# First chunk of a CIN tower: rows of x by transposes on the chip instead of a trip through DRAM

## The chip, the cores and the metric

The kernel runs on one core of one Trainium2 chip. The metric is the device time of the kernel in microseconds (us). Every line number L123 is a line of the kernel before.

## The reference, cut to what matters

For each of 512 samples, 32 table rows of 32 floats are gathered by `ids`. They form x[b, h, d], with field h and embedding dimension d. Two CIN layers follow, then a small tower.

```
z   = einsum('bhd,bmd->bhmd', x, x)        # layer 0: 32 x 32 pairs of fields
x1  = relu(einsum('b(hm)d,(hm)n->bnd', z, filter_0))      # n = 128
z   = einsum('bhd,bmd->bhmd', x, x1)       # layer 1: 32 x 128 pairs
x2  = relu(einsum('b(hm)d,(hm)n->bnd', z, filter_1))
h   = concat([sum_d x1, sum_d x2, dense_ctx])             # 512 x 272
y   = relu(relu(h @ W_top1 + b_top1) @ W_top2 + b_top2) @ W_top3
```

## The kernel before, in words

**Chunks and tiles.** The work is cut into 32 chunks c. A chunk is 128 samples (block bt = c // 8) times 4 embedding dimensions, so it has 512 columns. Each chunk has four tiles q, one for each dimension, and there are 128 tiles in all.

**Layer 0 of a chunk.** The pairs of fields are rows of up to 128, and a "product" is one row of x (repeated) times another. Symmetric pairs are folded, so there are four products k = 0 to 3 of 128 rows and one small one. VectorE (DVE) multiplies (`product`, L562), ScalarE (ACT) rounds the product to fp32r (`split_high`, L453), and DVE takes the rest (`split_low`, L567). TensorE (PE) then runs three fp32r passes per product (`three_passes`, L700 to L702) into the accumulator `acc0`. The small rows take one pass (`layer0_rest`, L723). After that ACT writes `prev_hi` (L465) and DVE writes `prev_lo` (L571).

**Where the rows come from.** ACT sorts the gathered block by dimension (`sort_d`, L431), PE transposes it (`turn_x`, L709) and ACT copies it to `xt_stage` (L440). SyncE (SP) writes it to a DRAM scratch `xt` (`write_xt`, L245 and L246) and reads it back three times with repeated rows: `load_xm` (L251), `load_xb` (L256) and `load_x16` (L263). ACT copies `xm` to PSUM (`copy_xm`, L446). The queue of SP runs in program order, and loads wait until the product that read the buffer is done.

**Layer 1 of a chunk.** It consists of 8 banks for each tile. A bank is three passes of 512 columns, four fields by 128 outputs. Four or five banks of a tile go to `ya` and are scaled by ACT (`scale_bank`, L473, four ACTIVATEs for each bank) and summed by GpSimd (POOL) and an accumulating DMA (`halve`, L313, and `sum_up`, L320). The other three or four go to `yd` and are scaled and summed by DVE (`add_bank`, L614), with a lag of three tiles. So the first three tiles of chunk 0 have only ACT banks. `ya` has two buffers and `yd` has three.

**Order.** All queues are written out by hand in the order (chunk c, tile q, bank j). Layer 0 of chunk c + 1 lies between the banks of chunk c. Layer 0 of chunk 0 lies ahead of everything. POOL gathers the 32 fields of block 0, then 22 of block 1 (`EARLY_NEXT`), and the other 74 gathers lie one at a time between its sums in chunks 0 to 19. ACT sorts block 1 within chunk 5, after a wait for all its gathers. On DVE the low half of filter 1 (`w1_lo`, L551) is made ahead of layer 0 of chunk 0.

## Time and profile before

| | us |
|---|---|
| three runs | 913.08, 915.85, 915.92 (median 915.85) |
| profiled execution, its own time | 913.09 |
| its span, first to last instruction | 911.1 |
| first bank of layer 1 starts at | 80.65 |
| first `yd` bank starts at | 101.31 |

The span has three parts. In the first part x is gathered and layer 0 of chunk 0 is made, up to the first bank. The second part holds three tiles whose banks all go to ACT. In the third part both consumers work and TensorE is busy without a break until the tail.

### The profile page before, as it was taken

To read this page: it belongs to the slowest core of one execution; us is meant where nothing else is said; L and a number is where in the kernel's file an instruction comes from. 1 tells how busy PE (TensorE), PEld (TensorE's weight loads), DVE (VectorE), ACT (ScalarE), POOL (GpSimd) and SP (SyncE) were. 2 spreads that over 40 slices of the span, in tenths; PEclk is the share of its full clock that TensorE was granted. 3 is DMA by queue.
4 is the path that set the end of the run, shared out by engine and by line. 5 is a ranking of instruction groups with operands and counts; after the bars stand their busy time and mean duration, and the time that the engine had idled before them with its cause. 6 is when DMAs were issued, how large, how long until landed. Compare 5 with 4: busy or idle time off the path is not lost.

```text
span 911.1 us, 14406 instructions
## 1 busy us (share of the span) xinstructions
PE 834.5 (92%) x3580; PEld 669.8 (74%) x3580; DVE 762.5 (84%) x2394; ACT 766.9 (84%) x2577; POOL 666.2 (73%) x633
## 2 busy tenths in 40 slices
PE   0316999999999999999999999999999999999997
PEld 0113788887888888887888788887888888888773
DVE  0213699998999999998999999998999999999774
ACT  0314999999999999999999999999999999999872
POOL 6773688787879887886888888866676666676580
PEclk9998999999999999999999999999999999999999
DMA  9144766776766766768766767667676676665430
GB/s 268 19 108 129 168 149 155 163 170 166 171 150 150 164 156 155 159 145 189 164 155 143 165 144 166 157 153 169 151 168 159 153 158 154 145 155 117 79 65 0
DMA packets 57575, 133.32 MB, mean 146 GB/s; under 512 B 8770, under 2 KB 22306, under 8 KB 57395
## 3 DMA queue, kind: packets, MB, share of 16 engines
q0 software_dynamic: 22384, 68.70, 41.8%
q1 hardware_dynamic: 32178, 59.94, 20.3%
q10 hardware_dynamic: 2928, 3.76, 1.4%
q8 instruction: 28, 0.46, 0.2%
q14 instruction: 57, 0.46, 0.1%
HBM read 62.64 MB, written 5.24 MB: 75 GB/s over the span
## 4 chain that ended last, share of the span: by engine, by line
PE 84%; ACT 5%; POOL 4%; issue 3%; DVE 2%; DMA 1%; SPq 0%; DVEq 0%
PE ya L700 14%; PE ya L702 14%; PE ya L701 14%; PE yd L700 10%; PE yd L702 10%; PE yd L701 10%; ACT scaled L473 4%; POOL emb L297 4%; PE acc L700 3%; PE acc L702 3%; PE acc L701 3%; DMA x<-xt_scratch 1%; DVE acc L614 1%; PE acc L723 1%; PE yd L813 1%
## 5 line engine op out<-in xcount | busy, mean ns | idle before, releaser
L473 ACT ACTIVATE scaled<-ya,emb 128x128 f32<-128x128 f32 x2312 | 664.0, 386 | 56.3 <-PE ya L702 49.3
L614 DVE SCALAR_TENSOR_TENSOR acc<-yd,emb,acc 128x128 f32<-128x128 f32 x1400 | 395.2, 342 | 7.6 <-PE yd L702 7.2
L320 POOL TENSOR_TENSOR quarter<-scaled 128x512 f32<-128x512 f32 x127 | 194.3, 1530 | 61.5 <-DMA scaled<-scaled 33.2
L700 PE MATMUL ya<-w_hi,prev_hi 128*128 128x512 f32 x578 | 228.6, 396 | 11.3 <-ACT scaled L473 5.7
L701 PE MATMUL ya<-w_lo,prev_hi 128*128 128x512 f32 x578 | 225.9, 391 | 0.0
L702 PE MATMUL ya<-w_hi,prev_lo 128*128 128x512 f32 x578 | 225.8, 391 | 0.0
L313 POOL DMA_DIRECT2D scaled<-scaled x127 | 117.1, 922 | 101.5 <-ACT scaled L473 94.7
L700 PE MATMUL yd<-w_hi,prev_hi 128*128 128x512 f32 x446 | 174.7, 392 | 0.6 <-DVE pooled_b L639 0.6
L702 PE MATMUL yd<-w_hi,prev_lo 128*128 128x512 f32 x446 | 173.6, 389 | 0.0
L701 PE MATMUL yd<-w_lo,prev_hi 128*128 128x512 f32 x446 | 173.6, 389 | 0.0
L297 POOL DMA_INDIRECT emb<-in_tbl,idx x128 | 135.2, 1056 | 30.1 <-issue 26.9
L700 PEld LDWEIGHTS ya<-w_hi,prev_hi 128*128 128x128 f32 x578 | 108.9, 188 | 42.1 <-ACT scaled L473 13.7
L702 PEld LDWEIGHTS ya<-w_hi,prev_lo 128*128 128x128 f32 x578 | 108.9, 188 | 23.1
L701 PEld LDWEIGHTS ya<-w_lo,prev_hi 128*128 128x128 f32 x578 | 109.1, 189 | 21.6
L562 DVE TENSOR_TENSOR prod<-xb,xm_ps 128x512 f32<-128x512 f32 x128 | 87.8, 686 | 31.7 <-issue 28.3
L614 DVE SCALAR_TENSOR_TENSOR acc<-yd,emb,part 128x128 f32<-128x128 f32 x254 | 77.1, 345 | 40.0 <-PE yd L702 35.7
L328 POOL TENSOR_TENSOR part<-quarter 128x256 f32<-128x256 f32 x127 | 99.4, 783 | 10.0
L700 PEld LDWEIGHTS yd<-w_hi,prev_hi 128*128 128x128 f32 x446 | 83.7, 188 | 19.4 <-DVE pooled_b L639 1.4
L567 DVE TENSOR_TENSOR lo<-prod,hi 128x512 fp32r<-128x512 f32 x128 | 87.3, 682 | 11.5 <-ACT hi L453 9.5
L701 PEld LDWEIGHTS yd<-w_lo,prev_hi 128*128 128x128 f32 x446 | 83.7, 188 | 17.9 <-issue 0.5
L702 PEld LDWEIGHTS yd<-w_hi,prev_lo 128*128 128x128 f32 x446 | 83.7, 188 | 17.5
L324 POOL TENSOR_TENSOR quarter<-quarter,scaled 128x512 f32<-128x512 f32 x65 | 84.2, 1295 | 5.1
(81 smaller groups left out, 719.0 us busy)
## 6 DMA issues: line engine op xcount, KB each, us to landing
scaled<-scaled POOLq DMA_DIRECT2D x127, 512.0 KB, 5.9
xb<-xt_scratch SPq DMA_DIRECT2D x64, 512.0 KB
x<-xt_scratch SPq DMA_DIRECT2D x64, 192.0 KB
xm<-xt_scratch SPq DMA_DIRECT2D x32, 256.0 KB
emb<-in_tbl,idx POOLq DMA_INDIRECT x128, 4.4
scaled<-in_L_rec_filter SPq DMA_DIRECT2D x8, 256.0 KB
xt_scratch<-xt_stage SPq DMA_DIRECT2D x7, 256.0 KB
xt_scratch<-xt_stage SPq DMA_DIRECT2D x9, 128.0 KB
```

Source lines behind the costliest of these rows:

```text
L297: pool.indirect_dma_start(emb[:, bt, D * f:D * (f + 1)], None, tables[f], bass.IndirectOffsetOnAxis(ap=idx[:, bt, f:f + 1], axis=0)).then_ ...
L313: pool.dma_start(piece[:, 0:2 * C], piece[:, 2 * C:4 * C], accum_op=ALU.add).then_inc(halved[tile % PR], 16)
L320: pool.tensor_tensor(four, piece[:, 0:C], piece[:, C:2 * C], ALU.add).then_inc(quartered, 1)
L324: pool.tensor_tensor(four, four, piece[:, 4 * C:5 * C], ALU.add).then_inc(quartered, 1)
L328: pool.tensor_tensor(part[:, tile % PR].rearrange("p i n -> p (i n)"), four[:, 0:2 * N], four[:, 2 * N:4 * N], ALU.add).then_inc(part_read ...
L473: op = act.activation(scaled[:, tile % PR, C * j + N * i:C * j + N * (i + 1)], ya[:, n % RA, N * i:N * (i + 1)], ACT.Copy, scale=scale_of( ...
L562: dve.tensor_tensor(prod[:], xb[:, k, :], xm_ps[:], ALU.mult).then_inc(product_ready, 1)
L567: dve.tensor_tensor(lo[:, n % 2, :], prod[:], hi[:, n % 2, :].bitcast(F32), ALU.subtract).then_inc(lo_ready, 1)
L614: dve.scalar_tensor_tensor(after, y_part, scale_of(tile, HB * j + i), before, ALU.mult, ALU.add).then_inc(chained, 1)
L700: pe.matmul(dst, v_hi, m_hi, start=start, stop=False)
L701: pe.matmul(dst, v_hi, m_lo, start=False, stop=False)
L702: return pe.matmul(dst, v_lo, m_hi, start=False, stop=stop)
```

## The change

Chunk 0 no longer reads its rows of x from DRAM. ACT copies the gathered fields of block 0, dimensions 0 to 3, into two SBUF tiles: `fields_up` (fields in order, four positions apart, started at 0, 4, 8 and 12) and `fields_four_times` (each field four times). DVE adds the last eight fields to the first. PE transposes slices of them in seven groups of four into PSUM (`turn_first`). Two of the results are copied to SBUF by ACT, and DVE multiplies five products from them. PE multiplies each by whole fp32 filter rows, one fp32 product instead of three fp32r passes. `turn_x` for the loads of chunk 1 comes after the seventh group, and its second half after the first product.

The scratch no longer gets chunk 0. SP writes chunks 1 to 3, then 4 to 7, and then loads chunks 1 and 2. The `w1_lo` subtractions on DVE come after the five multiplications. Layer 0 of chunk 1 moves: its products start inside tile 1 of chunk 0 instead of tile 0, the small product goes from POOL to DVE and is multiplied by PE last, and its loads of `xm` go to a buffer of their own with no copy to PSUM. `EARLY_NEXT` falls from 22 to 13, so nine gathers of block 1 move in between the tiles. Counts of semaphores move by one chunk throughout (one example is shown).

The diff, cut to its core:

```diff
     EARLY = 3 * F // 4
-    EARLY_NEXT = 22
+    EARLY_NEXT = 13
     GATHER_CHUNKS = 20
     assert (F, D, N, B % P, DC) == (32, 32, 128, 0, 4)
...
         emb = sb("emb", [P, BT, F * D])
+        fields_up = sb("fields_up", [P, DC, 4 * (F + 4)])
+        fields_four_times = sb("fields_four_times", [P, DC, 4 * F])
...
         w16 = scaled_flat[0:3 * F, (F + 2 * KT) * N:(F + 2 * KT + 1) * N]
+        first_product = scaled_flat[:, (F + 2 * KT + 2) * N:(F + 2 * KT + 2) * N + (KT + 1) * C].rearrange(
+            "p (t c) -> p t c", t=KT + 1)
+        first_x = scaled_flat[:, 8192:8192 + C]
+        first_x_once = scaled_flat[0:F, 8192 + C:8192 + 2 * C]
+        next_x = scaled_flat[:, 8192 + 2 * C:8192 + 3 * C]
         quarter = sb("quarter", [P, 2, C])
...
+        first_rows = [yd[:, 0, :], yd[:, 1, :], yd[:, 2, :], prod[:], xm_ps[:]]
...
+        def first_emb(fields):
...
             def load_xm(c):
-                if c > 0:
-                    sp.wait_ge(xm_in_psum, c)
-                sp.dma_start(xm[:], dram(xt, c * CH, [[C, F], [0, 4], [1, C]])).then_inc(xm_loaded, 16)
+                if c > 2:
+                    sp.wait_ge(xm_in_psum, c - 2)
+                sp.dma_start(next_x if c == 1 else xm[:], dram(xt, c * CH, [[C, F], [0, 4], [1, C]])).then_inc(xm_loaded, 16)
...
             def load_xb(c, r):
-                if c > 0:
-                    sp.wait_ge(product_ready, KT * (c - 1) + 2 * r + 2)
+                if c > 1:
+                    sp.wait_ge(product_ready, KT * (c - 2) + 2 * r + 2)
                 sp.dma_start(xb[:, 2 * r:2 * r + 2, :], dram(xt, c * CH + 2 * C * r, [[C, F], [KT * C, 4], [1, 2 * C]])
...
             sp.wait_ge(a_used, 1)
-            write_xt(0, 0, 2, xt_first_written)
+            write_xt(0, 1, 4, xt_first_written)
+            sp.wait_ge(a_used, 2)
+            write_xt(0, 4, CPB)
             sp.wait_ge(xt_first_written, 32)
-            load_l0(0)
             load_l0(1)
-            sp.wait_ge(a_used, 2)
-            write_xt(0, 2, 4)
-            write_xt(0, 4, CPB)
-            sp.wait_ge(xt_written, 64)
-            for c in range(2, CHUNKS):
+            load_l0(2)
+            sp.wait_ge(xt_written, 32)
+            for c in range(3, CHUNKS):
                 bt = c // CPB
                 if c % CPB == 0:
                     sp.wait_ge(a_used, turn_number(bt, 1) + 1)
                     write_xt(bt, 0, 4)
                     write_xt(bt, 4, CPB)
-                    sp.wait_ge(xt_written, 64 * (bt + 1))
...
-            small_product(1)
             for c in range(CHUNKS):
-                if c + 1 < CHUNKS:
+                if 0 < c < CHUNKS - 1:
...
+            def repeat_four_times(fields):
+                once = first_emb(fields)
+                act.activation(fields_four_times[:, :, 4 * fields.start:4 * fields.stop].rearrange("b d (f i) -> b d f i", i=4),
+                               bass.AP(once.tensor, once.offset, [list(dim) for dim in once.ap] + [[0, 4]]),
+                               ACT.Copy).then_inc(four_times_ready, 1)
+            def spread_up(i, fields, at):
+                act.activation(fields_up[:, :, 4 * at + i:4 * (at + fields.stop - fields.start - 1) + i + 1:4],
+                               first_emb(fields), ACT.Copy).then_inc(fields_up_ready, 1)
             act.wait_ge(gathered_first, 16 * EARLY)
+            for i in range(4):
+                spread_up(i, slice(4 * i, EARLY), 0)
+                spread_up(i, slice(0, 4 * i + 4), F - 4 * i)
+            repeat_four_times(slice(0, EARLY))
             sort_d(0, slice(0, EARLY))
             act.wait_ge(gathered[0], 16 * (F - EARLY))
+            repeat_four_times(slice(EARLY, F))
             sort_d(0, slice(EARLY, F))
+            act.wait_ge(first_turned, 1)
+            act.activation(first_x, xm_ps[:], ACT.Copy).then_inc(first_x_copied, 1)
+            act.wait_ge(first_turned, 3)
+            act.activation(first_x_once, acc0[0:F], ACT.Copy).then_inc(first_x_copied, 1)
             stage_xt(0, 0)
             stage_xt(0, 1)
-            copy_xm(0)
-            split_high(0, 0)
-            small_high(0)
-            for k in range(1, KT):
-                split_high(0, k)
             prev_high(0)
             for c in range(CHUNKS):
...
                             sort_d(bt, slice(F * j // SORT_PARTS, F * (j + 1) // SORT_PARTS))
-                        if (c, q) == (0, 0):
-                            if j == 0:
-                                copy_xm(1)
-                            if j == 1:
+                        if c == 0:
+                            if (q, j) == (1, 0):
                                 split_high(1, 0)
-                            if j == 2:
+                            if (q, j) == (1, 2):
                                 split_high(1, 1)
-                            if j == 3:
+                            if (q, j) == (1, 4):
+                                split_high(1, 2)
+                            if (q, j) == (2, 0):
                                 small_high(1)
+                            if (q, j) == (2, 1):
+                                split_high(1, 3)
...
             dve.tensor_tensor(low_third, w16[2 * F:3 * F], low_third.bitcast(F32), ALU.subtract).then_inc(w_lo_ready, 1)
-            for s in range(2):
-                dve.wait_ge(w_hi_ready, 3 + s)
-                fields = slice(s * F // 2, (s + 1) * F // 2)
-                dve.tensor_tensor(w1_lo[:, fields, :], w1_raw[:, fields, :], w1_hi[:, fields, :].bitcast(F32),
-                                  ALU.subtract).then_inc(w_lo_ready, 1)
...
-                if k == 0:
-                    dve.wait_ge(xm_in_psum, c + 1)
+                n = KT * (c - 1) + k
+                if k == 0 and c == 1:
+                    dve.wait_ge(xm_loaded, 16)
+                if k == 0 and c > 1:
+                    dve.wait_ge(xm_in_psum, c - 1)
                 if k % 2 == 0:
-                    dve.wait_ge(xb_loaded[k // 2], 16 * (c + 1))
+                    dve.wait_ge(xb_loaded[k // 2], 16 * c)
                 if n > 0:
                     dve.wait_ge(lo_ready, n)
-                dve.tensor_tensor(prod[:], xb[:, k, :], xm_ps[:], ALU.mult).then_inc(product_ready, 1)
+                dve.tensor_tensor(prod[:], xb[:, k, :], next_x if c == 1 else xm_ps[:], ALU.mult).then_inc(product_ready, 1)
...
-            def first_small():
-                dve.wait_ge(x16_loaded, 32)
+            def spread_up_last():
+                n = F - EARLY
+                last = first_emb(slice(EARLY, F))
+                to = fields_up[:]
+                dve.tensor_copy(bass.AP(to.tensor, 4 * (EARLY - 12) + 3, [list(to.ap[0]), list(to.ap[1]), [15, 4], [4, n]]),
+                                bass.AP(last.tensor, last.offset, [list(last.ap[0]), list(last.ap[1]), [0, 4], list(last.ap[2])])
+                                ).then_inc(fields_up_ready, 1)
+            def multiply_first(t):
+                if t == 0:
+                    dve.wait_ge(first_x_copied, 1)
+                if t == KT:
+                    dve.wait_ge(first_x_copied, 2)
+                dve.wait_ge(first_turned, FIRST_TURN[t])
+                if t < KT:
+                    product = dve.tensor_tensor(first_product[:, t, :], first_rows[t], first_x, ALU.mult)
+                else:
+                    product = dve.tensor_tensor(first_product[0:F, t, :], first_rows[t][0:F], first_x_once, ALU.mult)
+                product.then_inc(first_multiplied, 1)
+            def small_product(c):
+                dve.wait_ge(x16_loaded, 32 * c)
+                if c > 1:
+                    dve.wait_ge(small_lo_ready, c - 1)
                 dve.tensor_tensor(small[:], x16[:, 0, :], x16[:, 1, :], ALU.mult).then_inc(small_ready, 1)
-                dve.wait_ge(small_hi_ready, 1)
+            def small_low(c):
+                dve.wait_ge(small_hi_ready, c)
                 low_third = small_split[0:F]
                 dve.tensor_tensor(low_third, small[0:F], low_third.bitcast(F32), ALU.subtract).then_inc(small_lo_ready, 1)
-            def small_product(c):
-                dve.wait_ge(x16_loaded, 32 * (c + 1))
-                dve.wait_ge(small_lo_ready, c)
-                dve.tensor_tensor(small[:], x16[:, 0, :], x16[:, 1, :], ALU.mult).then_inc(small_ready, 1)
...
-            product(0, 0)
-            first_small()
-            for k in range(KT):
-                split_low(0, k)
-                if k + 1 < KT:
-                    product(0, k + 1)
+            dve.wait_ge(gathered[0], 16 * (F - EARLY))
+            spread_up_last()
+            for t in range(KT + 1):
+                multiply_first(t)
+            for s in range(2):
+                dve.wait_ge(w_hi_ready, 3 + s)
+                fields = slice(s * F // 2, (s + 1) * F // 2)
+                dve.tensor_tensor(w1_lo[:, fields, :], w1_raw[:, fields, :], w1_hi[:, fields, :].bitcast(F32),
+                                  ALU.subtract).then_inc(w_lo_ready, 1)
             prev_low(0)
             add_to_sum0(0)
             product(1, 0)
             split_low(1, 0)
             product(1, 1)
+            split_low(1, 1)
+            product(1, 2)
+            small_product(1)
+            split_low(1, 2)
+            product(1, 3)
+            small_low(1)
             for c in range(CHUNKS + 1):
...
                                 join_chains(tile)
-                        if j == 0 and (q < 3 and c + 1 < CHUNKS):
+                        if j == 0 and (q < 3 and c + 1 < CHUNKS) and (c > 0 or q == 2):
                             split_low(c + 1, q + 1)
                         if j == 0 and (q == 3 and c + 2 < CHUNKS):
                             split_low(c + 2, 0)
-                        if j == 2 and (q < 2 and c + 1 < CHUNKS):
+                        if j == 2 and (q < 2 and c + 1 < CHUNKS) and c > 0:
                             product(c + 1, q + 2)
                         if j == 2 and (q >= 2 and c + 2 < CHUNKS):
                             product(c + 2, q - 2)
-                        if (q, j) == (2, 1) and c < GATHER_CHUNKS:
+                        if (q, j) == ((3, 2) if c == 0 else (2, 1)) and c < GATHER_CHUNKS:
                             small_product(c + 2)
...
+            def turn_first(dst, source, columns):
+                rows = len(range(*columns.indices(source.shape[2])))
+                for d in range(DC):
+                    turn = pe.transpose(dst[0:rows, P * d:P * (d + 1)], source[:, d, columns], identity[:])
+                turn.then_inc(first_turned, 1)
...
+            pe.wait_ge(ctx_share_ready, H1 // P)
+            pe.wait_ge(four_times_ready, 2)
+            turn_first(xm_ps[:], fields_four_times, slice(0, P))
+            pe.wait_ge(fields_up_ready, 9)
+            turn_first(first_rows[0], fields_up, slice(0, P))
+            turn_first(acc0[:], fields_four_times, slice(0, P, 4))
+            for t in range(1, KT):
+                turn_first(first_rows[t], fields_up, slice(4 * t, 4 * t + P))
+            pe.wait_ge(first_x_copied, 2)
+            turn_first(first_rows[KT], fields_up, slice(19, 4 * (F + 4), 4))
             pe.wait_ge(sorted_d, 2)
             turn_x(0, 0)
-            turn_x(0, 1)
-            pe.wait_ge(w_lo_ready, 2)
-            for k in range(KT):
-                layer0(0, k)
-            layer0_rest(0)
+            for t in range(KT):
+                pe.wait_ge(first_multiplied, t + 1)
+                if t == 1:
+                    turn_x(0, 1)
+                pe.matmul(acc0[:], w0_a[:, t, :], first_product[:, t, :], start=t == 0, stop=False)
+            pe.wait_ge(first_multiplied, KT + 1)
+            pe.matmul(acc0[:], w16[0:F], first_product[0:F, KT, :], start=False, stop=True).then_inc(l0_done, 1)
             pe.wait_ge(w_lo_ready, 4)
-            pe.wait_ge(ctx_share_ready, H1 // P)
             for c in range(CHUNKS + 1):
                 if c < CHUNKS:
...
                             bank_d(tile, j)
-                    if (c, q) == (0, 0):
-                        layer0(1, 0)
-                    if q < 3 and c + 1 < CHUNKS:
+                        if (c, q, j) == (0, 1, 2):
+                            layer0(1, 0)
+                        if (c, q, j) == (0, 2, 1):
+                            layer0(1, 2)
+                    if (c, q) == (0, 1):
+                        layer0(1, 1)
+                    if q < 3 and c + 1 < CHUNKS and (c > 0 or q == 2):
                         layer0(c + 1, q + 1)
```

## Rows read from the trace of the kernel before

**Rows 1.** The page of the profile: span, and busy time of each engine.
```profile
span 911.1 us, 14406 instructions
...
PE 834.5 (92%) x3580; PEld 669.8 (74%) x3580; DVE 762.5 (84%) x2394; ACT 766.9 (84%) x2577; POOL 666.2 (73%) x633
```

**Rows 2.** Busy time of each engine by stage: us from:to, length, then each engine.
```profile
80.00:100.00 20.00, 15.78 (x50) 9.73 (x51) 6.54 (x10) 16.06 (x55) 3.79 (x4) 0.88 0.51 131
...
110.00:135.00 25.00, 25.00 (x112) 20.69 (x111) 24.14 (x77) 23.44 (x81) 21.50 (x21) 1.00 0.69 160
```

**Rows 3.** The timeline up to the first product: start, duration, engine, line.
```profile
25.16 4.49 DVE L551 TENSOR_TENSOR w_lo<-scaled,w_hi 128x2048 fp32r<-128x2048 f32 x2 [1.27 <-issue]
...
25.39 7.16 PE L696 MATMUL yd<-ctx_t,wt_ctx 16*128 16x512 f32 x8 [12.71 <-issue]
...
37.01 0.84 ACT L431 ACTIVATE emb_sorted<-emb 128x768 f32<-128x768 f32 x1 [3.74 <-DMA emb<-in_tbl,idx]
...
44.54 0.94 POOL L297 DMA_INDIRECT emb<-in_tbl,idx  x1 [0.30 <-issue]
...
46.81 0.42 ACT L431 ACTIVATE emb_sorted<-emb 128x256 f32<-128x256 f32 x1 [8.95 <-DMA emb<-in_tbl,idx]
...
47.28 1.97 PE L709 MATMUL ya<-identity,emb_sorted 128*128 128x128 f32 x8 [14.73 <-ACT emb_sorted L431]
...
48.43 0.60 ACT L440 ACTIVATE xt_stage<-ya 128x512 f32<-128x512 f32 x1 [1.20 <-PE ya L709]
49.05 0.37 SPq L245 DMA_DIRECT2D xt_scratch<-xt_stage  x1
...
51.65 0.56 SPq L251 DMA_DIRECT2D xm<-xt_scratch  x1
...
57.83 0.70 DVE L562 TENSOR_TENSOR prod<-xb,xm_ps 128x512 f32<-128x512 f32 x1 [28.18 <-issue]
...
64.10 0.69 DVE L587 TENSOR_TENSOR small<-x 96x512 f32<-96x512 f32 x1 [5.57 <-issue]
...
66.91 0.77 PE L700 MATMUL acc<-hi,w_hi 128*128 128x512 f32 x1 [17.66 <-issue]
```

**Rows 4.** The timeline from the last product of layer 0 to the second tile group.
```profile
74.58 0.45 PE L723 MATMUL acc<-small_split,w_split 96*128 96x512 f32 x1
...
79.08 0.60 ACT L465 ACTIVATE prev_hi<-acc 128x512 fp32r<-128x512 f32 x1 [6.71 <-remote]
...
80.65 0.76 PE L700 MATMUL ya<-w_hi,prev_hi 128*128 128x512 f32 x1 [5.62 <-DVE prev_lo L571]
...
82.31 1.14 ACT L473 ACTIVATE scaled<-ya,emb 128x128 f32<-128x128 f32 x4 [2.64 <-PE ya L702]
...
85.06 0.50 PE L700 MATMUL ya<-w_hi,prev_hi 128*128 128x512 f32 x1
...
101.31 0.39 PE L700 MATMUL yd<-w_hi,prev_hi 128*128 128x512 f32 x1
```

**Rows 5.** Busy time by stage around the end of layer 0 of chunk 0.
```profile
74.00:77.00 3.00, 1.03 (x3) 0.40 (x2) 0.00 (x0) 0.00 (x0) 0.00 (x0) 1.00 1.02 329
77.00:80.00 3.00, 0.00 (x0) 0.00 (x0) 0.29 (x1) 0.60 (x1) 1.25 (x1) 0.68 0.25 85
```

**Rows 6.** The four context products, 16 rows deep: nanoseconds least/median/most.
```profile
L696 PE MATMUL yd<-ctx_t,wt_ctx x8: 1056/1056/1187, 25.4 to 31.5; 16*128 16x512 f32 x8
```

**Rows 7.** The timeline of TensorE at the end of the kernel.
```profile
899.06 7.13 PE L813 MATMUL yd<-scaled,wt_sb 128*128 128x512 f32 x16 [0.84 <-ACT scaled L529]
```

**Rows 8.** The timelines of POOL and ACT at the start of chunk 5.
```profile
205.26 1.07 POOL L297 DMA_INDIRECT emb<-in_tbl,idx  x1 [0.16 <-issue]
...
208.26 0.43 ACT L431 ACTIVATE emb_sorted<-emb 128x256 f32<-128x256 f32 x1
```

**Rows 9.** The table of waits from 110 to 500 us: total, times, longest.
```profile
POOL quarter L320 <- DMA scaled<-scaled: 23.0, 14, 3.2
...
POOL scaled L313 <- ACT scaled L473: 21.9, 20, 3.6
```

More of the change, by code:

```diff
@@ L135, in cin_tower @@
         gathered = [sem(f"gathered_{t}") for t in range(BT)]
+        fields_up_ready = sem("fields_up_ready")
+        four_times_ready = sem("four_times_ready")
+        first_turned = sem("first_turned")
+        first_x_copied = sem("first_x_copied")
+        first_multiplied = sem("first_multiplied")
         sorted_d = sem("sorted_d")
@@ L227, in dram @@
             return bass.AP(tensor.tensor, offset, dims)
+        def first_emb(fields):
+            return emb[:, 0, D * fields.start:D * fields.stop].rearrange("b (f d) -> b d f", d=D)[:, 0:DC]
         block = ctx.enter_context(nc.Block())
@@ L259, in load_x16 @@
             def load_x16(c):
-                if c > 0:
-                    sp.wait_ge(small_ready, c)
+                if c > 1:
+                    sp.wait_ge(small_ready, c - 1)
                 for s in range(2):
@@ L286, in _ @@
                     write_xt(bt, 4, CPB)
-                    sp.wait_ge(xt_written, 64 * (bt + 1))
+                    sp.wait_ge(xt_written, 64 * bt + 32)
                 load_l0(c)
@@ L354, in small_product @@
             def small_product(c):
-                pool.wait_ge(x16_loaded, 32 * (c + 1))
-                pool.wait_ge(small_lo_ready, c)
+                pool.wait_ge(x16_loaded, 32 * c)
+                if c > 1:
+                    pool.wait_ge(small_lo_ready, c - 1)
                 pool.tensor_tensor(small[:], x16[:, 0, :], x16[:, 1, :], ALU.mult).then_inc(small_ready, 1)
             def small_low(c):
-                pool.wait_ge(small_hi_ready, c + 1)
+                pool.wait_ge(small_hi_ready, c)
                 low_third = small_split[0:F]
@@ L380, in _ @@
                             gather(bt, f, gathered[bt])
-                    if q == 1 and GATHER_CHUNKS <= c < CHUNKS - 2:
+                    if GATHER_CHUNKS <= c < CHUNKS - 2 and q == 1:
                         small_product(c + 2)
@@ L455, in small_high @@
             def small_high(c):
-                act.wait_ge(small_ready, c + 1)
-                if c > 0:
+                act.wait_ge(small_ready, c)
+                if c > 1:
                     act.wait_ge(l0_done, c)
@@ L519, in _ @@
                                 copy_xm(c + 2)
-                            if (q, j) == (3, 3):
+                            if (q, j) == (3, 3 if c > 0 else 4):
                                 small_high(c + 2)
@@ L710, in turn_x @@
                 turn.then_inc(a_ready, 1)
+            def turn_first(dst, source, columns):
[3 more added lines that the diff above has]
+                turn.then_inc(first_turned, 1)
             def layer0(c, k):
-                n = KT * c + k
-                if k == 0 and c > 0:
+                n = KT * (c - 1) + k
+                if k == 0:
                     pe.wait_ge(prev_hi_ready, c)
```

18 lines of the change are left out of this document (10 added, 8 removed).

## The prediction

> **What bounds the kernel now.** I read the page first. TensorE (PE) is busy for 834.5 of 911.1 us [rows 1]. That is an average, so I then read the busy time by stage. From 110 us on, PE is busy 25.00 of 25.00 us. From 80 to 100 us it is busy only 15.78 of 20, while ACT is busy 16.06 [rows 2]. The third view is the timeline of the start. It shows a first part up to 80.65 us with almost no work on PE, then three tiles that pace ACT, and the first `yd` bank at 101.31 us [rows 4]. From there to the tail PE sets the time, and the change leaves the number of its passes there alone. So the question is by how much the `yd` bank at 101.31 moves forward. Everything behind it should move with it.
>
> In the first part, the last of 32 gathers is issued at 44.54 and ACT sees it at 46.81. By 48.43 the block is sorted, turned and on its way to `xt_stage`. SP starts to write at 49.05 and to load at 51.65. DVE gets its first operands at 57.83 and the small rows at 64.10, so PE starts layer 0 only at 66.91 [rows 3]. It then goes around the loop of ACT, DVE and PE four times, to 75.03. The first bank starts at 80.65 [rows 4]. From the last gather seen to the first bank 33.8 us pass.
>
> **Ahead of the last gather.** ACT gains eight `spread_up` copies of at most 96 elements per partition and one repeat of 384. Its sort of 256 elements took 0.42 us and that of 768 took 0.84 [rows 3]. So the eight cost at most 8 x 0.42 = 3.4 us and the repeat at most 0.84. They start with the sort at 37.01 and end with it by 42.1, and ACT then waits until 46.81. Cost: nothing, with 4.7 us of cover.
>
> **From the last gather to the first product.** At 46.81 ACT repeats the last eight fields, 128 elements (four such pieces of L473 took 1.14 us [rows 4], so 0.29), and DVE spreads the same at about the same price. No row has DVE's stepped copy. Its bounds are 0 and 0.70 (512 elements, L562 [rows 3]), and 0.3 is nearest, beside ACT's. PE starts to turn at 47.15. Eight transposes took 1.97 us, and ACT followed the first four after 1.15 [rows 3]. So a first group costs 1.12 and each later one (1.97 - 1.12) = 0.85, at the low clock. There are seven groups, and then the first half of `turn_x`.
>
> The clock is the open term. PE had worked since 80.65 when its passes fell from 0.76 to 0.50 us at 85.06 [rows 4]. A whole fp32 product of 512 columns takes 7.13 / 8 = 0.89 us at the end of the kernel [rows 7], at the full 2.4 GHz, and 7.16 / 4 = 1.79 in the context products [rows 3], at 1.2 GHz. Taking the same 4.4 us of work, the full clock comes at 51.5. Then:
> - groups 1 to 5 end at 47.15 + 1.12 + 4 x 0.85 = 51.7, and groups 6, 7 and the half turn, at 0.45 each, at 53.0
> - five products at 0.89 and the second half turn at 0.45 take 4.9, so layer 0 ends at 57.9.
>
> The multiplications on DVE lie beside it. The first waits for the copy of `first_x` (48.3 + 0.6) and starts at 49.2. Each takes 0.70, and the last waits for group 7 (52.6) and ends at 53.4, so PE never waits for them. The moved `w1_lo` is 4.49 us [rows 3], from 53.4 to 57.9. It is hidden by the products on PE and by ACT's 0.60 for `prev_hi`, which ends at 58.55, so its cover is 0.7 us. Should DVE be late by more, it delays `prev_low`, the first bank and thus everything by as much.
>
> From ACT's `prev_hi` to the first bank took 80.65 - 79.08 = 1.57 us [rows 4]. So the first bank starts at 57.95 + 1.57 = 59.5, which is 21.1 us earlier.
>
> **The three ACT tiles.** They took 101.31 - 80.65 = 20.66 us [rows 4]. The ACT work among them is the same, four high halves and one small one, but for `copy_xm(1)`, 0.60 (as L440, [rows 3]). With the clock already full, the first bank also reaches ACT after about 1.2 instead of 82.31 - 80.65 = 1.66. That gives 19.6, and the `yd` bank starts at 79.1, 22.2 us earlier.
>
> **Are the loads of chunk 1 there?** `turn_x(0, 0)` ends at 53.0, and the ACT copy ends at 53.7, where SP writes 288 KB. The second half follows at 55.05 with 384 KB and two more issues, until 56.4. The load of `xm` took 2.60 us after the first write (49.05 to 51.65) and had less to write then. I take 56.8. DVE had its operands 6.2 us after that, and the small rows 12.45 after (57.83 and 64.10 against 51.65 [rows 3]). The 384 KB in front add 1.2 at the 329 GB/s of [rows 5]. So `xb` is there at 64.2 and `x16` at 70.5. ACT asks for the first product after the fifth bank, at 60.7 + 5 x 1.15 = 66.4, and DVE asks for the small rows at about 72. The margins are 2.2 and 1.5 us. Cost: nothing. Behind a late `xb` would stand ACT's `split_high(1, 0)`, and behind that all banks.
>
> **POOL.** It loses two small-row operations of chunk 1 to an idle DVE. With 13 early gathers it is free at 44.54 + 13 x 1.25 + 1 = 62, before tile 0 is scaled. With 22 it would hold `halve(0)` until 73. The nine gathers go in between later tiles, and each costs 1.07 + 0.16 us [rows 8], 11 in all. From 110 to 500 us POOL waits 23.0 us for its DMA and 21.9 for ACT [rows 9], so it has room for them. I take 0 of a possible 11. One deadline gets tight. With 13 early, the last gather of block 1 is the one in the position of the row at 205.26. ACT saw the 44.54 gather 2.27 us after issue, which makes 207.5 here, and ACT sorts at 208.26 [rows 8]. The margin is 0.7 us. A miss would cost its lateness once.
>
> **The sum.** 21.1 + 0.6 + 0.5 = 22.2 us. The profiled execution took 913.09 with a span of 911.1, so about 2 us lie around the span. It stands at the low end of the three runs, whose median is 915.85. From its own time the sum gives 890.9, from the median 893.6. I take **893**.
>
> **The clock, once more.** The context products were busy for 7.16 us without a break, and the last still took 1056 ns for each instruction, as the first [rows 6]. They use 16 of 128 rows. So being busy alone did not raise the clock, and transposes may not either. If only the real products count, the eight groups run low (to 54.2), as do two products and the half turn (to 58.6), and three products at 0.89 end at 61.3. The first bank starts at 62.9, and the gain is 17.7 + 1.1 = 18.8.
>
> The Trainium skill, page "TensorE: Matmul & The Clock Gate", section "What's actually happening", says that the throttled clock is the default and that sustained matmul activity releases it. By it alone the transposes count and the sum stays 22.2. The context rows do not agree with it for shallow products. No row shows transposes long enough.
>
> **Rivals.**
> - *The clock rises late or not at all before the first bank.* For it: [rows 6]. Against it: the transposes are 128 rows deep. As just worked out the gain is 18.8, so 897. All low, the products end at 54.2 + 5 x 1.79 + 0.85 = 64.0 and the gain is 15, so 900.5.
> - *The hole comes back.* The last small product is recorded until 75.03, yet ACT starts at 79.08 and is put down to "remote" [rows 4]. DVE, ACT and POOL stand idle while the DMA engines are full at a share of 1.02 [rows 5]. My timeline has no such 4 us. The new one has a like burst of writes from 54 to 57, and if it delays PE's release there the gain is 18.2 and the time 897.
> - *Chunk 1's rows are late.* If its loads take half as long again behind the writes, ACT waits 1 to 4 us for `xb` and DVE as much for `x16`. That costs 3 to 6, so 896 to 899.
> - *POOL.* The late gather or bursts of two gathers in a tile cost 1 to 5 us, so 894 to 898.
> - *Slower than before.* One mechanism could do it, the wait of ACT for `xb` of chunk 1. It decides once `xb` comes more than 22 us after 66.4, that is at 88.4, 31 us after its issue against the 6.2 of the rows. At 35 us the time is about 919.
>
> **How the numbers follow.** I give the forecast 0.53, the late clock 0.18, the hole 0.12, the late rows 0.10, POOL 0.05 and slower 0.02. The forecast's own range is 890 to 896, from the two starting points. The rivals on the same side reach 900.5, and together with them a range of 889 to 900 leaves out less than 2 in 10. A change within 0.3%, about what a measurement of this kernel can tell from none, needs a loss of nearly all 22 us. Faster gets 0.97, same 0.01, slower 0.02.
>
> **What the profile after would show.** Transposes should start at about 47.2, and the seventh group should end by 52.6 if the clock rose, by 53.4 if it did not. The first whole product should take 0.89 against 1.79. `prev_hi` at 58 and the first bank at 59.5 confirm the sum. If ACT sits idle in tile 1 before `hi` and the releaser is a DMA or the `prod` of DVE, the loads are late. PE must be busy throughout from the first `yd` bank at about 79 on. If not, POOL's rows in chunks 0 to 19 would have `quarter` or `part` waited for by DVE. DVE's `w_lo` must end before ACT's `prev_hi`, or the 0.7 us of cover was not enough. The prediction is wrong if the first `yd` bank comes at 79 and the end has moved by less than that.

## The result, and the profile after

The kernel after takes 906.34 us (median of four runs, 904.40 to 908.24). Timed beside it, the kernel before takes 915.0 (four runs, 913.08 to 915.92). The ratio is 0.9907 [0.989, 0.9924], so it is faster by 0.9%, or 8.7 us. The prediction said 893, a gain of 22.

The page of the kernel after, beside [rows 1]:

```profile
span 906.4 us, 14442 instructions
...
PE 843.7 (93%) x3605; PEld 673.0 (74%) x3605; DVE 761.2 (84%) x2392; ACT 766.0 (85%) x2582; POOL 663.4 (73%) x631
```

TensorE's busy time grew by 9.2 us. The same two kernels on another chip (before_c and after_c, below) differ by 0.9 (835.7 and 836.6), so most of this is not work that the change adds, but work that ran slower. The timeline of the kernel after, from the last gather to the first `yd` bank and then in the tail, beside [rows 3, 4, 7]:

```profile
45.42 0.31 ACT L499 ACTIVATE fields_four_times<-emb 128x128 f32<-128x128 f32 x1 [7.26 <-DMA emb<-in_tbl,idx]
...
47.60 1.06 PE L776 MATMUL acc<-identity,fields_four_times 128*32 128x128 f32 x4
...
48.46 1.63 PE L776 MATMUL yd<-identity,fields_up 128*128 128x128 f32 x8
...
54.95 0.59 ACT L520 ACTIVATE scaled<-acc 32x512 f32<-32x512 f32 x1 [7.35 <-remote]
...
55.59 1.04 PE L776 MATMUL xm_ps<-identity,fields_up 128*32 128x128 f32 x4 [5.06 <-issue]
...
57.27 1.91 PE L831 MATMUL acc<-scaled 128*128 128x512 f32 x2
...
59.37 0.95 POOL L315 DMA_INDIRECT emb<-in_tbl,idx  x1 [0.30 <-issue]
64.74 0.69 DVE L633 TENSOR_TENSOR scaled<-yd,scaled 128x512 f32<-128x512 f32 x1 [16.13 <-remote]
...
66.40 4.61 PE L831 MATMUL acc<-scaled 128*128 128x512 f32 x6
...
68.66 4.47 DVE L701 TENSOR_TENSOR w_lo<-scaled,w_hi 128x2048 fp32r<-128x2048 f32 x2
...
72.09 0.60 ACT L484 ACTIVATE prev_hi<-acc 128x512 fp32r<-128x512 f32 x1 [3.97 <-PE acc L833]
73.06 0.67 DVE L604 SCALAR_TENSOR_TENSOR prev_lo<-acc,prev_hi 128x512 fp32r<-128x512 f32 x1
...
73.99 0.77 PE L761 MATMUL ya<-w_hi,prev_hi 128*128 128x512 f32 x1 [1.94 <-DVE prev_lo L604]
...
92.50 0.40 PE L761 MATMUL yd<-w_hi,prev_hi 128*128 128x512 f32 x1
...
892.72 8.83 PE L895 MATMUL yd<-scaled,wt_sb 128*128 128x512 f32 x16 [0.84 <-ACT scaled L565]
```

Two holes are to be seen. ACT waits at L520 only for the third group of transposes. The profile has that group done at 48.66, yet ACT starts at 54.95. DVE's second multiplication needs the fourth group, which was recorded within the 1.63 us from 48.46, and it starts at 64.74. Both waits are put down to "remote", which means that the profile could name no releaser. The semaphore records in the trace say more. Of the seven increments that TensorE makes behind the seven groups, five are recorded, and those of the third and the fourth group stand at 54.92 and 64.72. That is 6.3 and 15.2 us after the last transposes of these groups ended (48.66 and 49.52), and ACT and DVE start 0.03 and 0.02 us behind them. The increments of ACT and DVE themselves came within 0.01 us of the end of the instruction (47.59 and 47.60, 65.43 and 65.44). So the engines that wait are not slow. The signal of TensorE comes late. The increments of the last three groups stand at 66.83 to 66.95, and the fifth, whose transposes ended at 50.09, kept DVE's third multiplication waiting for 1.4 us more.

The stages of the kernel after, by windows (columns as in [rows 2], with the granted clock after the engines and then DMA share and GB/s):

```profile
45.80:50.60 4.80, 4.65 (x24) 4.19 (x24) 0.69 (x1) 0.83 (x2) 3.59 (x4) 1.00 0.11 14
50.60:55.50 4.90, 0.00 (x0) 0.00 (x0) 0.00 (x0) 0.56 (x1) 3.78 (x4) 0.75 0.09 13
55.50:59.20 3.70, 3.60 (x10) 1.83 (x10) 0.00 (x0) 0.03 (x1) 2.84 (x3) 0.50 0.12 13
59.20:65.40 6.20, 0.00 (x0) 0.00 (x0) 0.66 (x1) 0.00 (x0) 0.95 (x1) 0.78 0.04 5
65.40:72.10 6.70, 6.57 (x12) 2.84 (x12) 5.28 (x6) 1.09 (x3) 0.00 (x0) 0.65 0.46 115
```

In both holes hardly anything computes, and the DMA engines are nearly empty (0.09 and 0.04). In the first, POOL issues a gather every 1.25 us. The second begins as POOL issues the last of these gathers, at 59.37, and goes on for 5.4 us behind that. The clock falls to its lower level (1.2 GHz) within each hole, and its mean is 0.50 in the stage behind the first and 0.65 in that behind the second.

The gain goes as follows. The first bank comes 6.66 us earlier than in [rows 4] (80.65 to 73.99). The `yd` bank comes 8.81 earlier (101.31 to 92.50), since the three ACT tiles took 18.51 us in place of 20.66. The last `yd` bank is added at 889.67 against 896.01, so 6.34 are left there. The 16 instructions of [rows 7] took 8.83 us instead of 7.13, because the clock fell to its lower level in the tail (from 892.8 to 896.2), and the span is 4.7 us shorter.

### The profile page after: what moved, and what is told of

It is laid out like the page before. It is cut to its first block, busy times and chain, and to the rows that moved or that the text cites. A ratio compares the mean times of both kernels' runs of the same rounds, so it can differ in the third digit from the quotient of the medians.

```text
span 906.4 us, 14442 instructions
## 1 busy us (share of the span) xinstructions
PE 843.7 (93%) x3605; PEld 673.0 (74%) x3605; DVE 761.2 (84%) x2392; ACT 766.0 (85%) x2582; POOL 663.4 (73%) x631
## 3 DMA queue, kind: packets, MB, share of 16 engines
q1 hardware_dynamic: 31324, 58.14, 19.8%
## 4 chain that ended last, share of the span: by engine, by line
PE 76%; POOL 7%; DVE 4%; ACT 4%; DMA 3%; issue 3%; another core or an unknown queue 2%; POOLq 0%; DVEq 0%
PE ya L761 13%; PE ya L763 12%; PE ya L762 12%; PE yd L761 9%; PE yd L763 9%; PE yd L762 9%; POOL emb L315 4%; ACT scaled L492 3%; DMA scaled<-scaled 3%; PE acc L761 3%; PE acc L762 3%; PE acc L763 3%; DVE acc L666 2%; POOL quarter L338 1%
## 5 line engine op out<-in xcount | busy, mean ns | idle before, releaser
L338 POOL TENSOR_TENSOR quarter<-scaled 128x512 f32<-128x512 f32 x127 | 196.9, 1550 | 63.5 <-DMA scaled<-scaled 49.7
L331 POOL DMA_DIRECT2D scaled<-scaled x127 | 120.1, 946 | 111.3 <-ACT scaled L492 105.4
L315 POOL DMA_INDIRECT emb<-in_tbl,idx x128 | 132.1, 1032 | 29.5 <-issue 19.7
L600 DVE TENSOR_TENSOR lo<-prod,hi 128x512 fp32r<-128x512 f32 x124 | 84.4, 681 | 6.9 <-ACT hi L472 6.8
L595 DVE TENSOR_TENSOR prod<-xb,xm_ps 128x512 f32<-128x512 f32 x120 | 82.1, 684 | 1.1 <-ACT xm_ps L465 0.8
```

The source lines that it names most:

```text
L315: pool.indirect_dma_start(emb[:, bt, D * f:D * (f + 1)], None, tables[f], bass.IndirectOffsetOnAxis(ap=idx[:, bt, f:f + 1], axis=0)).then_ ...
L331: pool.dma_start(piece[:, 0:2 * C], piece[:, 2 * C:4 * C], accum_op=ALU.add).then_inc(halved[tile % PR], 16)
L338: pool.tensor_tensor(four, piece[:, 0:C], piece[:, C:2 * C], ALU.add).then_inc(quartered, 1)
L595: dve.tensor_tensor(prod[:], xb[:, k, :], next_x if c == 1 else xm_ps[:], ALU.mult).then_inc(product_ready, 1)
L600: dve.tensor_tensor(lo[:, n % 2, :], prod[:], hi[:, n % 2, :].bitcast(F32), ALU.subtract).then_inc(lo_ready, 1)
```

## The experiments

After the first measurement the kernels ran in six sets, on six different chips, and each set has the kernel before timed beside them. Which chip the first measurement ran on is not on record. I call a trace *with holes* when it shows "remote" waits like the two above.

| set | kernel: us (runs) | before, us | holes |
|---|---|---|---|
| first measurement | after 906.34 (4) | 915.0 | yes |
| 1 | warm44 887.54, full_columns 890.1, gathers_later 897.77, two_sems 890.46 (1 each) | 911.37 | none |
| 2 | after_again 905.99 (4), before_again 912.74 (1) | 914.09 | both |
| 3 | after_b 892.45 (1), two_sems_b 889.9 (4), warm44_b 889.4 (4) | 911.25 | none |
| 4 | after_c 890.57, warm44_c 890.42, before_c 911.2 (1 each) | 910.78 | none |
| 5 | gathers_later_d 900.32, warm44_d 886.77, full_columns_d 891.68 (1 each) | 911.12 | none |
| 6 | after_e 906.67 (4), warm44_e 910.45 (5), gathers_later_e 899.7 (1) | 914.87 | first two; none in the third |

### Set 1: four ways to close the holes

The first edit, warm44, keeps TensorE busy ahead of the transposes with 44 products whose result is not used:

```diff
+            pe.wait_ge(w_hi_ready, 2)
+            for _ in range(44):
+                pe.matmul(ya[:, 0, :], w0_hi[:, 0, :], w0_hi[:].rearrange("p t n -> p (t n)"), start=True, stop=True)
             pe.wait_ge(four_times_ready, 2)
```

> 44 idle fp32r passes of 128 rows x 512 columns stand ahead of the first transpose, so that TensorE works from about 33 us until the last gather is seen. Theory A (the completions of TensorE are held back around its clock's rise out of a cold start, and the clock falls again in the hole): the rise and any hole now lie ahead of 45 us; transposes at 0.11 us each, prev_hi at about 55, first bank by 58, time 890 to 893. Theory B (few-column transposes hold the completions), C (gather traffic), D (two engines waiting on one semaphore): the holes of 5 and 6 us stay, first bank at 70 or later, time 902 to 908.

The second, full_columns, lets groups 3 and 7 of the transposes use all 128 columns instead of 32 (the rows of chunk 0 are then not the right ones):

```diff
-            turn_first(acc0[:], fields_four_times, slice(0, P, 4))
+            turn_first(acc0[:], fields_four_times, slice(0, P))
...
-            turn_first(first_rows[KT], fields_up, slice(19, 4 * (F + 4), 4))
+            turn_first(first_rows[KT], fields_up, slice(16, 16 + P))
```

> The third and the seventh group transpose 128 columns instead of 32 (the wrong rows, so the outputs are not the reference's). Theory B (completions are held behind a transpose with 32 columns): both holes go, first bank at about 58 to 62, time 890 to 896. Theories A, C, D: holes stay, first bank at 70 or later, time 902 to 908.

The third, gathers_later, takes all gathers of block 1 away from the start of the kernel and puts two of them into each of the first tiles, then one:

```diff
-    EARLY_NEXT = 13
+    EARLY_NEXT = 0
...
-            per_tile = [len(later) * k // (DC * GATHER_CHUNKS) for k in range(DC * GATHER_CHUNKS + 1)]
+            per_tile = [min(2 * k, 16 + k) for k in range(DC * GATHER_CHUNKS + 1)]
```

> No gather of block 1 is issued behind the 32 of block 0; they go two to a tile into tiles 0 to 15. Theory C (the gathers' transfers hold up TensorE's completions): holes go, first bank at 58 to 62. Theories A, B, D: first bank stays at 70 or later; the time stays at 902 to 908, give or take 1 us for fuller tiles on POOL.

The fourth, two_sems, gives the two groups that ACT waits for a semaphore of their own:

```diff
+        first_x_turned = sem("first_x_turned")
...
-            act.wait_ge(first_turned, 3)
+            act.wait_ge(first_x_turned, 2)
...
-                turn.then_inc(first_turned, 1)
+                turn.then_inc(done, 1)
```

> The groups that ACT waits for and those that DVE waits for count on two semaphores instead of one. Theory D (two engines waiting on one semaphore that TensorE counts up): holes go, first bank at 58 to 62. Theories A, B, C: first bank stays at 70 or later, time 902 to 908.

All four took 887.5 to 897.8, and no trace had a hole. Four unlike edits can't all be the cure, so the set told nothing apart. The kernel before was also faster here than in the first measurement, 911.37 against 915.0. That raised a new theory: the holes depend on the chip or the occasion. One cost did show. gathers_later is the slowest of the four, and its waits from 76 to 210 us (waiting instruction, releaser, us in total, times, longest) have a row that the kernel after has not:

```profile
DVE acc L666 <- POOL part L346: 8.8, 3, 3.1
```

### Sets 2 to 5: the same kernels again

Set 2 ran the two kernels unchanged.

> The changed kernel as it is. The four looks at edits of it had no hole, whichever edit was made, and none of the four theories named a cause that all four share. Theory E (the holes belong to the occasion: the same program has them in some executions or on some chips and not in others): first bank at 57 to 58, time 889 to 892, ratio to before about 0.977. Theory A, B, C and D in any mixture: holes as in the first measurement, first bank at 70 to 74, time 904 to 908.

> The kernel before as it is. Theory E: here too the 4.0 us between the last product of layer 0 and the ACT copy behind it are absent or different; without them the span is about 907 to 909. If the hole belongs to the program, the copy starts 4 us late again and the span is 911.

The holes are back: 905.99 against 914.09, ratio 0.9908 [0.9892, 0.9925], which repeats the first measurement. The kernel before has one too. Its timeline in before_again, beside [rows 4]:

```profile
72.38 0.94 POOL L297 DMA_INDIRECT emb<-in_tbl,idx  x1 [0.30 <-issue]
...
75.74 0.63 PE L723 MATMUL acc<-small_split,w_split 96*128 96x512 f32 x1
...
78.80 0.60 ACT L465 ACTIVATE prev_hi<-acc 128x512 fp32r<-128x512 f32 x1 [5.28 <-remote]
```

Set 3 went back to the kernel after, with two of the edits timed.

> The changed kernel again, on the same chip and occasion as the two that follow. Theory E (the holes belong to the chip or occasion): it has holes exactly if the two others have them. Theory F (they belong to the program, and each of the four edits happened to take them away): first bank at 73 and time 904 to 908 here, while the others have none.

> The two-semaphore edit again, timed. Theory E: like the changed kernel of this same call, so 904 to 908 if that one has holes and 889 to 892 if not. Theory F: 889 to 892 whatever the changed kernel does.

> The kernel with 44 idle passes ahead again, timed. Theory E: without holes 886 to 889; with holes between 895 and 906, as they then do not depend on the clock. Theory A (a cold start is what makes the holes) or F: 886 to 890 whatever the changed kernel does.

The unchanged kernel took 892.45, beside before at 911.25. Its first bank started at 58.19, where it started at 73.99 in the first measurement. The ratios are 0.9769 [0.9736, 0.9802] for two_sems_b and 0.9756 [0.9719, 0.9793] for warm44_b. So nothing here was cured by the edits: the kernel has no holes on this chip.

Set 4 looked at both kernels on one chip.

> Theory E (the holes belong to the occasion): if this call falls on an occasion without holes, the ACT copy behind layer 0 starts within 0.1 us of the last small product and the first bank at about 76 to 77, time 908 to 911; on the other kind it starts 2.5 to 4 us late, first bank at 80 to 81, time 912 to 915.

> Theory E: the same kind as the kernel before in this call: 889 to 893 without holes, 904 to 908 with them.

> On an occasion without holes 886 to 890. On one with holes: theory A (they hit a TensorE that starts cold) gives 886 to 892, theory E2 (they hit whatever TensorE issues after the first gathers, warm or not) 898 to 908 with one or two holes of about 5 us behind the first transposes.

The timeline of before_c:

```profile
75.34 0.63 PE L723 MATMUL acc<-small_split,w_split 96*128 96x512 f32 x1
76.01 0.60 ACT L465 ACTIVATE prev_hi<-acc 128x512 fp32r<-128x512 f32 x1 [2.89 <-PE acc L723]
...
77.59 0.76 PE L700 MATMUL ya<-w_hi,prev_hi 128*128 128x512 f32 x1 [1.62 <-DVE prev_lo L571]
...
98.28 0.39 PE L700 MATMUL yd<-w_hi,prev_hi 128*128 128x512 f32 x1
```

ACT follows the last small product after 0.67 us. In [rows 4] that took 4.5 us (74.58 to 79.08). The timeline of after_c:

```profile
45.44 1.09 PE L776 MATMUL xm_ps<-identity,fields_four_times 128*128 128x128 f32 x4 [12.61 <-ACT fields_four_times L499]
...
48.27 0.59 ACT L520 ACTIVATE scaled<-acc 32x512 f32<-32x512 f32 x1 [1.11 <-PE acc L776]
...
49.12 1.52 DVE L633 TENSOR_TENSOR scaled<-yd,scaled 128x512 f32<-128x512 f32 x2 [0.95 <-PE yd L776]
...
49.73 0.62 PE L776 MATMUL prod<-identity,fields_up 128*128 128x128 f32 x4
...
51.76 4.47 DVE L701 TENSOR_TENSOR w_lo<-scaled,w_hi 128x2048 fp32r<-128x2048 f32 x2
...
52.36 2.74 PE L831 MATMUL acc<-scaled 128*128 128x512 f32 x6
...
57.77 0.47 PE L761 MATMUL ya<-w_hi,prev_hi 128*128 128x512 f32 x1 [1.62 <-DVE prev_lo L604]
...
61.34 0.70 DVE L595 TENSOR_TENSOR prod<-xb,scaled 128x512 f32<-128x512 f32 x1 [3.23 <-DMA xb<-xt_scratch]
...
64.15 0.61 ACT L472 ACTIVATE hi<-prod 128x512 fp32r<-128x512 f32 x1
```

ACT and DVE follow the third and the fourth group within about 1.1 us of their start, and TensorE goes on without a stop. The first bank comes 19.8 us earlier than in before_c, the `yd` bank (75.78) 22.5 and the end of the span (888.8 against 909.2) 20.4.

Set 5 repeated three edits.

> For an occasion with holes. In both kernels they end 4 to 5 us after the last early gather has landed, and the semaphore records that are missing come back there. Theory C (the traffic of the back-to-back gathers is what TensorE's completions stand behind): with the gathers over at 45 us the holes are gone or shorter than 2 us in all, first bank by 60, time 896 to 900 (this edit costs some 7 us later on POOL, as seen without holes: 897.8). Otherwise holes of 10 us and more, time 908 to 914. On an occasion without holes 897 to 899, which tells nothing new.

> For an occasion with holes. Theory A (a TensorE that starts cold): 886 to 892. Otherwise 900 to 908. Without holes 886 to 891.

> For an occasion with holes. Theory B (the first signal held back is that of the group with 32 columns): 889 to 894. Otherwise 902 to 908. Without holes 889 to 892.

There were no holes again, so it couldn't tell apart what closes them. It repeats the order of set 1: 886.77, 891.68, 900.32.

### Set 6: the edits on a chip with holes

> The changed kernel, timed once more. Without holes 889 to 893 and a ratio of 0.977 to the kernel before; with them 904 to 908 and 0.991.

> Without holes 1 to 3 us below the changed kernel of this call: the transposes run at full clock from the first. With holes: theory A (cold start) 886 to 892, otherwise 898 to 908.

> Without holes 897 to 900. With holes: theory C (back-to-back gathers) 896 to 900 with the first bank by 60, otherwise 908 to 914.

The chip had holes. after_e gave 906.67, ratio 0.9911 [0.9895, 0.9928]. Its timeline has the two "remote" waits again:

```profile
56.48 0.59 ACT L520 ACTIVATE scaled<-acc 32x512 f32<-32x512 f32 x1 [9.74 <-remote]
...
64.18 0.69 DVE L633 TENSOR_TENSOR scaled<-yd,scaled 128x512 f32<-128x512 f32 x1 [16.43 <-remote]
```

The passes of warm44_e did not help. The kernel took 910.45 (908.22 to 912.39, five runs), ratio 0.995 [0.9928, 0.9971], which is slower than after_e. The timeline of TensorE in warm44_e:

```profile
33.25 11.27 PE L818 MATMUL ya<-w_hi 128*128 128x512 f32 x40 [0.78 <-issue]
46.65 0.40 PE L818 MATMUL ya<-w_hi 128*128 128x512 f32 x1 [2.13 <-issue]
49.44 0.59 PE L818 MATMUL ya<-w_hi 128*128 128x512 f32 x1 [2.39 <-issue]
52.24 0.59 PE L818 MATMUL ya<-w_hi 128*128 128x512 f32 x1 [2.21 <-issue]
...
59.94 0.37 PE L776 MATMUL xm_ps<-identity,fields_four_times 128*128 128x128 f32 x1 [2.43 <-issue]
62.74 0.37 PE L776 MATMUL xm_ps<-identity,fields_four_times 128*128 128x128 f32 x1 [2.43 <-issue]
63.44 0.47 PE L776 MATMUL xm_ps<-identity,fields_four_times 128*128 128x128 f32 x1 [0.34 <-issue]
64.14 0.47 PE L776 MATMUL yd<-identity,fields_up 128*128 128x128 f32 x1 [0.23 <-issue]
...
66.51 1.06 PE L776 MATMUL acc<-identity,fields_four_times 128*32 128x128 f32 x4
```

Forty of the 44 products run one behind another. The last four, which wait for nothing, and the transposes come one at a time, 2.1 to 2.8 us apart. Then they come 0.70 apart, and from 66.51 they run freely. POOL issues its last early gather at 58.57. Here the instructions themselves are held, while TensorE is not short of work. The first gap, from 44.52 to 46.65, came while the clock was still at its full level. It fell only at 47.6, within the hole. So a cold clock is not the cause. Nor is a group of 32 columns, or a semaphore of TensorE that two engines wait for, since neither came ahead of that gap.

gathers_later_e took 899.7 beside it, one run, against 906.67. Its timeline:

```profile
42.14 0.94 POOL L315 DMA_INDIRECT emb<-in_tbl,idx  x1 [0.30 <-issue]
44.62 0.31 ACT L499 ACTIVATE fields_four_times<-emb 128x128 f32<-128x128 f32 x1 [7.32 <-DMA emb<-in_tbl,idx]
...
48.08 0.59 ACT L520 ACTIVATE scaled<-acc 32x512 f32<-32x512 f32 x1 [1.28 <-PE acc L776]
...
48.76 0.69 DVE L633 TENSOR_TENSOR scaled<-yd,scaled 128x512 f32<-128x512 f32 x1 [0.94 <-PE yd L776]
...
58.19 0.77 PE L761 MATMUL ya<-w_hi,prev_hi 128*128 128x512 f32 x1 [1.62 <-DVE prev_lo L604]
...
76.71 0.40 PE L761 MATMUL yd<-w_hi,prev_hi 128*128 128x512 f32 x1
```

With no gathers behind 42.14 in this stretch, there is no hole on the chip that showed holes in the other two kernels. TensorE's increments behind the seven groups, six of which are recorded, came within 0.2 us of the groups' ends. This is one run. The first bank comes at 58.19, against 73.43 in after_e.

### What marks the two kinds of set

The engines' semaphore events can be counted in each trace:

```
chips with     before 10330  before_again 10493  after 10442  after_again 10478
holes          after_e 10410  warm44_e 10438  gathers_later_e 10421
chips without  before_c 11770  after_b 11689  after_c 11690  two_sems 11686, _b 11683
holes          full_columns 11690, _d 11689  gathers_later 11689, _d 11692
               warm44 11693, _b 11682, _c 11686, _d 11689
```

Some 1,250 to 1,440 events are missing on the chips with holes, most of them from the first 80 us (1,168 of 1,248 in after, counted against after_c), and more than nine in ten are events of DMAs (1,154 of these 1,248). They are missing long ahead of any hole: from 10 to 20 us after has 72 events and after_c 372. gathers_later_e lacks them as well, though it has no hole. So the missing events go with the chip and make no hole by themselves. As far as these runs go, the hole needs the chip and the gathers together. The timed runs of a set agree with its traced one: after took 904 to 908 us in all its twelve runs with holes, against 890.6 and 892.5 without. Each of the timed runs has a recorded span and clock as well, so no run here shows the kernel with the recording off.

## Why the prediction was wrong

**Where it failed.** The step is the sentence "My timeline has no such 4 us". With it I counted the gap of [rows 4] as gone, and gave the rival *the hole comes back* 4 us and a chance of 0.12. I had tied that rival to a burst of writes from 54 to 57, which the runs refute: both holes lie at DMA shares of 0.09 and 0.04. The rows that I had spoke against it too. In [rows 5] the share is 0.25 from 77 to 80, while the wait went on to 79.08. The hole did come back, several times as large. after_c gives its size, since it is the same kernel without it. From the first gather seen to the first bank it needs 57.77 - 44.99 = 12.78 us, and after needs 73.99 - 45.42 = 28.57. The 15.8 between them are:

- the first hole: the seventh group starts 10.17 after the gather instead of 5.20, so 5.0
- the second hole, in which TensorE stands still from 59.2 to 65.5: 6.3
- work at the lower clock: 1.7 between the holes (55.59 to 59.2, against 50.19 to 52.1 in after_c). Behind them, 0.5 in the half turn (0.91 to the next product against 0.43) and 1.9 in the products (5.7 from 66.40 against 3.8 from 52.36)
- `w_lo`, which ends at 73.13, so `prev_lo` starts at 73.06 and not right behind `prev_hi`: 0.3.

These add up to 15.7. Only the last two kinds belong to the prediction's terms.

**What holds TensorE up.** Shown, in one run on one chip with holes: taking away the gathers behind the transposes takes the holes away. Shown by warm44_e on the same chip: a warm clock does not, and the holding needs no group of 32 columns and no shared semaphore. The kernel before has neither in this stretch, and has a hole. Where there are holes, they end a like time after POOL has issued its last early gather: 6.8 us in before (72.29 to 79.08), 6.4 in before_again, 5.4 in after, 6.0 in after_again and 5.9 in after_e. In warm44_e it is 4.9 us to the quicker pace (63.44) and 7.9 to the free run (66.51). The change also put more of the path there. In before only ACT's step behind the last product waited; in after two steps in the midst of layer 0 wait, with work and a clock to lose behind each. Argued only: what links the two. In before, the products between 66.91 and 72.3 were not held, so a gather in flight does not stop every instruction. full_columns and two_sems were not run on a chip with holes. What differs between the chips, or whether the recording of the events has a part in it, stays open.

**The mechanism, step by step, on after_c.** The rest of the timeline held.

- *Layer 0* ended about 56.2 against 57.9, since the gather was seen 1.8 us earlier. The first bank came at 57.77 against 59.5.
- *The gain over before.* At the first bank it was 19.8 us, not 21.1. The 21.1 held the 4 us hole of before, which before_c does not have (77.59 instead of 80.65). The three ACT tiles gave it back: 18.0 us against the 19.6 that I took. So 22.5 us at the `yd` bank against 22.2 is right in part by luck, because these errors cancel.
- *`w1_lo`.* It ended at 56.23, and `prev_hi` at 56.79. The cover was 0.56, near the 0.7 of the forecast. In after it was short by 0.3, because there the products that should cover it started only when DVE released them.
- *Loads of chunk 1.* DVE read `xb` at 61.34, and ACT took the product only at 64.15. No cost in after_c. In after_b and full_columns_d the second `xb` came late, and TensorE waited 2.0 and 2.4 us for the third product (`yd` banks at 77.65 and 78.08). So the rival *chunk 1's rows are late* exists in some runs, at a little less than its 3 to 6 us.
- *POOL.* The nine gathers cost nothing that I can see there. From the `yd` bank to the last one added it took 797.9 us in after_c and 795.9 in before_c. TensorE was busy 1.1 us more (791.7 against 790.6), and its waits for ACT's `scaled` were 5.0 against 4.0 us. I did not find the cause of these 2 us. The edge is close by: two gathers to a tile cost 7 to 9 us (897.77 against 890.46 and 890.1 in set 1, 900.32 against 891.68 in set 5), as DVE waits for `part`.

**Sizes.** On chips without holes the change is worth 18.8 and 20.2 us (sets 3 and 4), and after takes 892.45 and 890.57. The range of 889 to 900 holds on those and fails on the chips with holes, where it is worth 8 to 9 us. No version beats the others on both kinds. Without holes warm44 is 0 to 5 us below after, two_sems and full_columns, and with them it is slower than after. gathers_later is nearly the same on both (898 to 900) and the best where there are holes. A version between the two, with a few early gathers and fewer tiles that hold two, would be next. It wasn't tried.

## What to carry to other kernels

An idle gap in the trace of before that no work of the kernel explains, here ACT "released by remote" 4 us after its operand was done, is to be priced as something that can move and grow with the code that takes its place, and not as one lump that is either there or gone. Ask what else was running when it ended. Before an experiment is believed to cure such a gap, run the unchanged kernel in the same set: four edits seemed to cure this one, and so did none at all.

## What the runs showed of the hardware

- On some chips TensorE's signals to other engines came late: by 2.4 us in before_again (76.37 to 78.77), 4.0 in before (75.03 to 79.05), 6.3 to 16.7 in after (50.09 to 66.83). The recorded increments of ACT and DVE in the same stretch of after came within 0.02 us. POOL issued one indirect gather every 1.25 us until 5 to 7 us before the hole ended. In warm44_e single instructions came 2.1 to 2.8 us apart, then 0.70, with nothing to wait for.
- The effect goes with the chip. The first measurement and two of the six chips of the sets showed it, for before as well, which took 914.1 to 915.0 us there and 910.8 to 911.4 on the four others.
- Whole fp32 products with 128 rows and 512 columns took 0.86 us each at full clock (0.43 between weight loads in after_c). A group of four fp32 transposes took 0.86 us at the lower clock and 0.46 at the full one.
- The clock went to full at 49.8 in after_c, after 4.3 us of fp32 transposes alone. The context products of [rows 6], busy for 7.16 us, kept 1056 ns for each instruction to the last.
